# List places sorted out by the top-eight instruction, and factors carried in the token rows

## The reference, cut to what matters

```
x = x + tanh(g_xattn) * attention(layernorm(x), ctx, ctx)
# mixture of experts, T = 4096 tokens, 64 scores a token: 32 routed experts and 32 "zero" experts
scores   = softmax(xf @ w_cls.T)
topk_idx = top_k(scores + bias, 8)
w        = scores[topk_idx] / (sum + 1e-20) * 1.5
routed   = topk_idx < 32
# each routed expert takes its tokens in order of arrival, at most CAP = 512 of them
y_e      = (silu(buf_e @ gate) * (buf_e @ up)) @ down
out      = sum over routed picks of w * y_e[token]   # times (1 + sum of w over zero experts)
x = x + tanh(g_ffn) * out
```

## Time and profile before

| what | value |
|---|---|
| median of 3 runs | 2238.2 us (2236.8 to 2238.26) |
| the profiled execution's own time | 2251.64 us |
| its span, first to last instruction | 2249.9 us |
| busy PE / DVE / ACT / POOL | 93% / 64% / 55% / 49% |
| granted TensorE clock, mean | 0.988 |
| DMA | 407.72 MB, mean 181 GB/s |

### The profile page before, as it was taken

The page is one execution under the profiler, slowest core; times in us unless marked ns, Lnnn a source line. Parts: engine busy times, 40 slices in busy tenths (PEclk is TensorE's granted clock), DMA queues, the critical chain, the costliest instruction groups (busy, mean ns, idle before and its releaser), DMA issues.

```text
span 2249.9 us, 48697 instructions
## 1 busy us (share of the span) xinstructions
PE 2088.6 (93%) x14808; PEld 1221.9 (54%) x14809; DVE 1451.2 (64%) x2463; ACT 1243.9 (55%) x1833; POOL 1092.2 (49%) x1246
## 2 busy tenths in 40 slices
PE   5999999988999787999999999999999999999997
PEld 2555455444544444456556564744656776554465
DVE  6788888888888582446446582843564875462475
ACT  3787777767776444335445473633464764353265
POOL 3127878887887576224323351622352644231255
PEclk9999999999999998999999999999999999999999
DMA  5477676665654764757666593965594986766574
GB/s 149 130 192 180 158 186 174 156 177 152 188 152 113 217 187 128 210 160 217 179 181 196 165 288 106 277 197 146 149 287 118 288 256 176 194 168 194 154 199 104
DMA packets 569847, 407.72 MB, mean 181 GB/s; under 512 B 214134, under 2 KB 489718, under 8 KB 569776
## 3 DMA queue, kind: packets, MB, share of 16 engines
q1 hardware_dynamic: 506112, 334.10, 51.4%
q0 software_dynamic: 46912, 72.10, 13.5%
q10 hardware_dynamic: 16752, 0.65, 0.5%
HBM read 321.43 MB, written 103.16 MB: 189 GB/s over the span
## 4 chain that ended last, share of the span: by engine, by line
PE 64%; DVE 15%; issue 11%; POOL 4%; ACT 3%; another core or an unknown queue 1%; SPq 1%; DMA 1%; DVEq 0%; POOLq 0%; ACTq 0%
PE psum L1684 33%; PE psum L1714 16%; DVE mx L1170 5%; PE psum L1571 5%; PE psum L1543 3%; PE psum L1556 3%; PE psum L1624 2%; DVE xgt L1337 2%; DVE wgu L1325 2%; DVE stats L1135 1%; POOL lists L726 1%; PE psum L1584 1%; DVE wdn L1330 1%; PE psum L1595 1%
## 5 line engine op out<-in xcount | busy, mean ns | idle before, releaser
L1684 PE MATMUL psum<-xgt,wgu 128*128 128x224 f16 (+3 forms) x6336 | 879.4, 296 | 30.7 <-DVE xgt L1337 13.5
L1684 PEld LDWEIGHTS psum<-xgt,wgu 128*128 (+1 forms) x6336 | 567.9, 98 | 341.0 <-issue 42.5
L809 POOL TENSOR_TENSOR spare<-spare 128x1 f32<-128x1 f32 x164 | 132.6, 808 | 794.8 <-PE psum L1714 425.4
L1714 PE MATMUL psum<-wdn,apair 128*128 128x512 f16 x1968 | 454.4, 381 | 15.1 <-issue 6.5
L1170 DVE TENSOR_REDUCE mx<-psum 128x2 f32<-128x512 f32 x512 | 327.6, 684 | 82.5 <-PE psum L1543 74.5
L1325 DVE SCALAR_TENSOR_TENSOR wgu<-wraw,wgu 128x1024 f16<-128x1024 f32 x264 | 318.7, 1218 | 42.3 <-ACT wgu L951 30.6
L726 POOL DMA_INDIRECT lists<-entry,dest x256 | 276.5, 1080 | 112.5 <-issue 70.0
L934 ACT ACTIVATE prob<-psum 128x512 f32<-128x512 f32 x512 | 277.3, 598 | 72.9 <-PE psum L1556 40.5
L1714 PEld LDWEIGHTS psum<-wdn,apair 128*128 128x128 f16 x1968 | 186.4, 98 | 219.1 <-issue 24.5
L1347 DVE SCALAR_TENSOR_TENSOR a<-psum,sg 128x512 f32<-128x512 f32 x132 | 90.9, 689 | 322.9 <-PE psum L1684 321.7
L1337 DVE COPY xgt<-psum 128x1024 f16<-128x1024 f16 x256 | 167.0, 684 | 199.7 <-PE psum L1624 194.8
(11 more groups left out here) (158 smaller groups left out, 1943.0 us busy)
## 6 DMA issues: line engine op xcount, KB each, us to landing
wraw<-in_L_ffn_w_gate_up_dram SPq DMA_DIRECT2D x264, 512.0 KB
wraw<-in_L_ffn_w_down_dram SPq DMA_DIRECT2D x132, 512.0 KB
x<-in_x_dram SPq DMA_DIRECT2D x16, 1024.0 KB
xr<-in_x_dram SPq DMA_DIRECT2D x16, 1024.0 KB
out_dram<-x SPq DMA_DIRECT2D x16, 1024.0 KB
pairs<-xs SPq DMA_DIRECT2D x16, 1024.0 KB
qs<-qh SPq DMA_DIRECT2D x248, 64.0 KB
qs<-ql SPq DMA_DIRECT2D x128, 64.0 KB
```

The costliest lines, as they stand in the source:

```text
L1684: mm = pe.matmul(ps_gu[:, s, h, 0:UP_COLUMNS[nt]], w[:, a, k, :], xgt[:, c, k, 0:UP_COLUMNS[nt]], start=(k == 0 and (a, c) == (0, 0)), sto ...
L1714: mm = pe.matmul(psum[:, Y_BANK[i] + n2, :], apair[:, o, k, c * P:(c + 1) * P], w[:, a, k, :], start=(k == 0 and (a, o) == (0, 0)), stop=( ...
```

## The change

- `hot`, `pick`, `picked`, `topi`, `topf`, `token` and everything that makes them go away: `max_index` and `topf` in `router_i`, `hot` in `positions`, `picks` on POOL, `entries_a` and `entries_b` on DVE.
- DVE gets `keys(b)` at the end of `positions` in slot 7 of step b+2: key = -place * mask, then one `dve.max` for each of the two token blocks. Its eight largest are the places of the routed picks (negated), and then zeros. POOL's `entries` turns them into `dest`; picks without a routed expert get a place out of bounds. POOL now runs `entries` for batches 13 to 15 too.
- The factor is no longer in the list. SP stores `coef` (256 pieces of 128 bytes a batch, `store_coefs`) beside the token rows, which grow from 4096 to 4224 bytes, and the gather brings them along into `xg`. POOL's new `keep(e)` copies the one factor column of the expert (128 x 4) to `cexp`, before `gather(e + 1)`. ACT's `y_out` reads `cexp` and waits for `coef_set`.
- New waits: `factors` and `router_w` wait until the store of the batch before has landed (`coefs_out`), since `coef` is one buffer. Waits on `entry_ready` in `router_b` and `router_i` become waits on `coef_ready`.

```diff
-    pairs = nc.dram_tensor("pairs", [ntok, 2 * H], F16).ap()
+    pairs = nc.dram_tensor("pairs", [ntok, XW // 2], I32).ap()      # XW = 2 * H + 2 * NROUTED
+    coefs_v = pairs[:, H:XW // 2].rearrange("(b t p) h -> b p t h", p=P, t=T2)
...
+            def store_coefs(b):                                       # SP
+                sp.wait_ge(coef_ready, b + 1)
+                sp.dma_start(coefs_v[b], coef[:].bitcast(I32)).then_inc(coefs_out, 16)
...
                 if on(b, -1):
                     store_x2(b - 1)
+                if on(b, -3) and b <= nb:
+                    store_coefs(b - 3)
...
                 if is_first(e):
                     for i in range(CHUNKS):
                         weights(1, i)
+                        if i in (1, 2):
+                            store_coefs(nb - 3 + i)
...
-            const(pool.iota(iota_e[:], ...))
+            const(pool.memset(entry[:], 0))
+            const(pool.memset(entry0[:], 0))
+            const(pool.iota(entry0[:, :, :, 0], pattern=[[S, 2], [P, T2]], base=(nb - 2) * S, channel_multiplier=1))
-            const(pool.iota(token[:], ...))
...
                 pool.wait_ge(mask_ready, b + 1)                        # factors
                 if b == 0:
                     pool.wait_ge(setup_dve, 2)
+                else:
+                    pool.wait_ge(coefs_out, 16 * b)
...
-            def picks(b, part):
...
             def entries(b, par):
+                pool.wait_ge(list_ready, T2 * (b + 1))
                 if b > 1:
                     pool.wait_ge(lists_out[par], 8 * T2 * TOPK * (b - par))
-                pool.tensor_scalar(dest[:, par], picked[:, 0], NO_SLOT, None, ALU.add).then_inc(pool_order, 1)
-                pool.tensor_copy(entry[:, par, :, 1].bitcast(F32), picked[:, 1]).then_inc(pool_order, 1)
-                pool_n[0] += 2
-                chain(pool.tensor_copy(entry[:, par, :, 0], token[:].rearrange("p t k -> p (t k)")))
-                pool.tensor_scalar(token[:], token[:], float(S), None, ALU.add).then_inc(entry_ready, 1)
+                chain(pool.tensor_scalar(dest[:, par], keyed[:, par].rearrange("p t k -> p (t k)"), -1.0, NO_SLOT, ALU.mult, ALU.add))
+                pool.iota(entry[:, par, :, 0], pattern=[[P, T2], [0, TOPK]], base=b * S, channel_multiplier=1).then_inc(entry_ready, 1)
...
+            def keep(e, par):                                          # POOL
+                if is_first(e):
+                    first_wait(pool)
+                else:
+                    pool.wait_ge(gathered, 16 * CT * e)
+                if not (isinstance(e, int) and e < 2):
+                    pool.wait_ge(y_free, 8 * (e - 1) + Y_FREE)
+                pool.tensor_copy(cexp[:, par], xgc[:, :, bass.ds(weights_of(e), 1)]).then_inc(coef_set, 1)
...
                     if at_step(b, nb):
+                        if kv == 2:
+                            keep(0, 0)
                         if kv in (2, 3):
                             scatter(b - 3, 1 - par, 9 * (kv - 2), 9 if kv == 2 else T2 * TOPK)
                     elif at_step(b, nb + 1):
                         if kv == 3:
                             scatter_first(b - 3)
+                            entries(b - 3, 1 - par)
                             scatter(b - 3, 1 - par, 0, 12)
                     elif early(b):
                         if kv == 3:
                             scatter_first(b - 3)
+                            entries(b - 3, 1 - par)
...
             def gather(e, par):
                 pool.wait_ge(gslots_in[par], 8 * e + 16 if par == 0 else 8 * (e + 1))
                 pool.wait_ge(gt_full, 8 * e)
+                if not (isinstance(e, int) and e == 1):
+                    keep(e - 1, 1 - par)
+                pool.wait_ge(coef_set, e)
...
+                if i == 0 and n2 == 0:                                 # ACT, y_out
+                    act.wait_ge(coef_set, e + 1)
-                               scale=slots[:, par, c, 1:2].bitcast(F32)).then_inc(y_free, 1)
+                               scale=cexp[:, par, c]).then_inc(y_free, 1)
...
                 for t in range(T2):                                    # DVE, router_i
-                    tally.add(dve.max_index(topi[:, t], top[:, t], biased[:, t]))
                     tally.add(dve.match_replace(left[:, t], top[:, t], biased[:, t], -1e30))
                 tally.wait()
                 dve.tensor_tensor(mask[:], left[:], biased[:], ALU.not_equal).then_inc(mask_ready, 1)
-                tally.add(dve.tensor_copy(topf[:], topi[:]))
...
                 dve.wait_ge(mask_ready, b + 1)                         # DVE, router_w
+                dve.wait_ge(coefs_out, 16 * b)
...
-                dve.tensor_tensor(hot[:].rearrange("p t k e -> p (t k) e"), ...,
-                                  ALU.is_equal).then_inc(list_ready, 1)
...
-            def entries_a(b, tally):
...
-            def entries_b(b, par, tally):
...
+            def keys(b, par, tally):                                   # DVE
+                dve.wait_ge(mask_ready, b + 1)
+                if apart(b):
+                    dve.wait_ge(first_ready, b - nb + 3)
+                if not is_first(b):
+                    dve.wait_ge(list_ready, T2 * b)
+                if not (isinstance(b, int) and b < 2):
+                    dve.wait_ge(entry_ready, b - 1 if isinstance(b, int) else b)
+                link(dve.scalar_tensor_tensor(out=key[:], in0=place[:], scalar=-1.0, in1=mask[:, :, 0:NROUTED],
+                                              op0=ALU.mult, op1=ALU.mult), tally)
+                carry_wait(tally)
+                for t in range(T2):
+                    dve.max(keyed[:, par, t], key[:, t]).then_inc(list_ready, 1)
...
                     if kv == 1 and at_step(b, nb - 2):
                         dve.wait_ge(x_full, of_q(nb - 1, "Q3"))
+                        dve.wait_ge(qlo_ready, 4 * nb)
                         dve.memset(xg[:], 0.0).then_inc(xg_clear, 1)
```

100 lines of the change are left out of this document (31 added, 69 removed).

## The result

On record: the kernel after takes 2205.05 us (median of 4 runs, 2199.74 to 2205.62), the kernel before 2237.5 us beside it; ratio 0.9853, 95% interval 0.9841 to 0.9866. My forecast was 2229 us, with a range down to 2217: the change brought 32.5 us, not 9.

A forecast was written before the change was run, and what follows sets the result against it. PE (64% of the chain) and DVE (15%) were taken to bound it, POOL only 4%. Loop 2.0 + 2 + 0.8, passage 5, start and experts 0: 9.8 us, 9.2 taken off 2238.2 gives 2229 us, range 2217 to 2242.

The forecast's parts named there:

- POOL's relief in the loop, 2.0 us for `veps` and 2 for the longest step: Attention loop: without picks POOL is some 6 us freer a step, winning 2.0 us at `veps`, 2 in the longest step.
- This buys time only where somebody waits for POOL", and "POOL meets its gates again: Attention loop: POOL's some 6 us matter only to waiters; then attention semaphores and ACT's `qf` gate POOL, scatters staying put.
- The median lies 13.4 us lower, for which I expect the same difference: Whole kernel: the 9.8 us summed on the 2251.64 us profile carry over to the median, 9.2 of it taken.
- POOL late in the longest loop step, 2 us: Longest loop step: POOL began `ql` 3.7 us late and DVE idled; the slack removes this, 2 us, between 0 and 6.
- `hot` to `keys`, 0.8 us: DVE in attention: `keys` at 0.55 us replaces `hot` at 0.61, gaining 0.06 a step, 0.8 in all (-3 to +4).
- `router_i` at nothing: DVE in attention: removing about 0.47 us of `max_index` and `topf` gains nothing, as DVE idles 1.88 behind; upper bound 6.
- SP's stores of the factors, 0 in the loop: SP in attention: 16 more DMAs of 32 KB land well before `factors` needs them; cost 0, bounds 0 and 6 us.
- The passage, 5 us: Between loop and experts: three PE waits for DVE shrink by 2.3, 1.69 and 2.07; 5 us taken, between 0 and 8.
- The experts, 0: Expert passes: `keep` before each of 32 gathers and 3% wider rows are covered, 0 us; without cover 32 us.
- The experts pay: Rival, 2245 us (12%): in 32 expert passes `keep` holds DVE or wider rows delay the gather; 0.5 a pass, 16 us.
- POOL was the hidden drag: Rival, 2210 us (12%): in the loop, picks cause 2.8 us a step, up to 28 us returning over ten steps.
- Nothing to see: Rival, 2237 us (22%): PE and ACT pace the loop, so it keeps its period; passage gains are lost in stalls.

The follow-up runs named there:

- e4_index_load: Kernel after with two max_index a batch and the cast topf put back on DVE: 2251.97 us, 1.0004 of before; control, kernel after unchanged: 2252.3 us.
- h1_one_product: Kernel after with one dummy product of 128 x 512 put back at the head of POOL's slot 0, no folding additions: 2217.65 us, 0.992 of before.
- f1_spread: Kernel after with one scatter instead of three in slot 5, three instead of one in slot 6, ahead of factors: 2220.38 us, 0.9932 of before.

## Why the prediction was wrong, step by step

- **POOL's relief in the loop, 2.0 us for `veps` and 2 for the longest step: the step that failed.** For `veps` I read 0.30 us, took 0.15 a step and 2.0 us in all, with 3.5 as bound. On kind A it is 1.61 us, slot 0 is 1.3 us longer on the mean, and the clock falls behind it, for which I had no term: slot 1 another 1.1. Ten steps of the loop: 470.0 - 442.8 = 27.2 us, step 13 another 3.7. The wait was the right one, its size was off by more than ten.
- **"This buys time only where somebody waits for POOL", and "POOL meets its gates again": the premise under it that failed.** POOL met hardly a gate in an ordinary step, in the very profile that I read: it waited 0.7 us for `qf` and 2.2 us for `veps` in six steps. I took its 4% of the chain for slack. With the picks gone it stands 4.4 us a step for `qf`, and the step is 2.9 us shorter. How the 27.2 us divide between the held `veps` with the clock behind it and the full POOL is open; the one product put back gives 15.8 us.
- **"The median lies 13.4 us lower, for which I expect the same difference": why it failed.** The 13.4 us were not an offset of the profiled execution: the profile is of kind B, on which the change is worth nothing, the median of kind A, on which it is worth 32.5 us. The 13.4 us themselves do not lie in the loop. At the end of step 13 the profile that I read is 5.7 us ahead of the one of kind A (687.25 and 692.91), at the down product of the third expert pass 14.4 us behind (955.28 and 940.85). On kind B DVE comes late to slot 0, since ACT and DVE have stood still in slots 3 and 5; so `veps` meets the product only at its end, and the long `veps` of kind A can't be seen there. That POOL had no time to spare could be seen. This last reason is read from the traces; what makes kind B slow in slots 3 and 5 beyond "it comes with the scatters" is open.
- **POOL late in the longest loop step, 2 us:** on kind A step 10 took 49.3 us, its neighbours 47.0; after, 44.0 as its neighbours. That is 2.3 us more than its neighbours gained. Right.
- **`hot` to `keys`, 0.8 us; `router_i` at nothing:** slot 7 stays at 5.28 to 5.29 in ordinary steps, so the 0.06 a step do not show; slot 5 4.24 to 4.23. The cover held on kind A, and on kind B in e4_index_load and its control.
- **SP's stores of the factors, 0 in the loop:** slots 2 and 3 keep their length. Right, as far as seen; what made PE wait for `mrow` in step 3, 1.85 us, is open.
- **The passage, 5 us:** from the end of step 13 (31.3 us ahead) to the fifth expert pass (33.8 ahead) it is 2.5 us. Of the three waits of PE in the earlier trace rows (on kind A they were 2.70, 3.24 and 0.60), the first and the last are gone, as forecast; the middle one is 1.09 and not 0, because DVE stood 2.44 us for the store of the factors, which I had held to be hidden ("if the landing took 10 us, 2 to 3 us would show"). The lead was 34.95 us at the down product and 31.4 at the next expert's first product, ahead of which PE waited 2.96 us for a gather (before: 0.97); from the fifth pass on it is 33.8.
- **The experts, 0:** the end of each pass lies 33.8 us before that of the kernel before from the fifth pass to the 31st, within 0.1. `keep` took 0.66 us on the mean, with idle time ahead of it. (The 4.36 us that I gave as the shortest of POOL's waits for the transposes ended with ACT's `ys`, not with them; the cover held all the same.) The 4224-byte rows cost nothing that shows. Right, and the rival *The experts pay* is out.
- **The rivals:** *POOL was the hidden drag* had the right size on kind A: I had priced it at 2.8 us a step from step 2, and it is 2.9 (47.0 - 44.1). My two reasons against it were weak: that the scatters stay is true, but without them the step is 43.0 (measured on kind B), so they are 1.1 us of it; and that POOL is 4% of the chain says nothing of DVE instructions that POOL stretches, since they stand in the chain as DVE. Its sign, "a step of 44 us or less", is what came. On kind B, where the step stayed at 46 us and more, *Nothing to see* is what came.

Open: why two kinds of chip; what the kernel before takes on kind A with the products behind `veps` and POOL as full as ever; why mixed columns win 0.5 to 0.6% on kind B though dropping all writes changes nothing (later scatters are a guess that was not tested there); whether spreading the train of slot 5 helps on kind B. No version tried beats the kernel after on kind A.

## What to carry to other kernels

A profile whose own time lies off the median of the plain runs, here by 0.6%, may show another bottleneck than theirs: look for the stretch that makes the difference before laying a sum on the median. A tiny DVE instruction that takes several times its usual length is a lead, even at 0.1 us: ask what happens to it when DVE comes a microsecond earlier. An engine with a small share of the chain can still set the pace: add up what it waits for in an ordinary step, and if that is nothing, it has no slack. And run the unchanged kernel beside each group of experiments; my first group was misread without it.

## What the runs showed of the hardware that I had not expected

- The same two kernels differ by 32.5 us on one kind of chip and by nothing on another.
- A DVE instruction that waits is not next in line: POOL's following product started 0.30 us after `veps` and held it another 1.28 us.
- In slot 0 on kind A an idle stretch of PE of 2.10 to 2.24 us was followed by the lower clock in nine steps of ten (before), one of 2.04 to 2.08 us in five of nine (h1_one_product), one of 1.74 to 1.76 us in two of eight (f1_spread), and one of 1.0 us in none (after). In h1_one_product each fall cost about 1.6 us; in the kernel before the one step without it was no shorter.
- With 16 indirect DMAs a step on kind B, engines that have no part in them come 2.6 us or more later a step (45.6 to 48 us against 43.0 without them). On kind A the step of the kernel after takes 44.1 us, at most 1.1 above the 43.0, which were measured on kind B.
